# Third mixture of a four-layer gated decoder: gate weights by way of memory, and later and earlier places for the steps around it

## The reference, cut to what matters

```python
x = x + tanh(g_xattn[2]) * _L2_xattn_ref(_layernorm(x), ctx, ...)   # product in the frequency domain (rfft, irfft)
x = x + tanh(g_ffn[2])   * _L2_ffn_ref(_layernorm(x), ...)          # the third mixture
x = x + tanh(g_xattn[3]) * _L3_xattn_ref(ctx, ctx, _layernorm(x), ...)
x = x + tanh(g_ffn[3])   * _L3_ffn_ref(_layernorm(x), ...)          # the last mixture
```

```python
scores = sigmoid(X @ gate_w.T)
_, idx = top_k(scores + bias, 4)
w = take(scores, idx); w = w / sum(w)
pos = cumsum(onehot(idx)) - 1; valid = pos < C        # C = 128 places per expert
h = silu(xe @ W1) * (xe @ W3);  ye = h @ W2           # per expert
out = sum over the 4 of ye * (w where valid) + silu(X @ sw1.T) * (X @ sw3.T) @ sw2.T
```

## Time and profile before

| | |
|---|---|
| median of 3 runs | 866.2 us (862.1 to 868.02) |
| the profiled execution | 867.06 us, its span 865.3 us |
| mean granted clock of TensorE | 0.939 |
| PE, DVE, POOL, ACT busy | 88%, 64%, 45%, 43% of the span |
| third mixture, first gate product to `out_back` | 536.03 to 728.22 us |
| DMA, mean over the span | 92 GB/s |

### The profile page before, as it was taken

The page is one execution under the profiler, slowest core; times in us unless marked ns, Lnnn a source line. Parts: engine busy times, 40 slices in busy tenths (PEclk is TensorE's granted clock), DMA queues, the critical chain, the costliest instruction groups (busy, mean ns, idle before and its releaser), DMA issues.

```text
span 865.3 us, 13644 instructions
## 1 busy us (share of the span) xinstructions
PE 759.5 (88%) x3936; PEld 539.0 (62%) x3936; DVE 553.4 (64%) x1813; ACT 375.8 (43%) x834; POOL 390.4 (45%) x381
## 2 busy tenths in 40 slices
PE   6989889999999878976979787999989989798995
PEld 3467767676767546654969786565645544555663
DVE  3377877777788378862633575978776655344554
ACT  0234344444445435625545334547455565313441
POOL 2000024544546434363674343655445665253772
PEclk8799989999999969966999998999999999899999
DMA  5021899930000121014677651000330000013325
GB/s 146 1 62 50 267 333 332 333 88 0 1 1 1 53 57 30 21 47 146 172 208 211 195 167 50 10 1 1 83 101 14 13 10 17 10 41 78 101 70 146
DMA packets 74394, 79.34 MB, mean 92 GB/s; under 512 B 17769, under 2 KB 61424, under 8 KB 74194
## 3 DMA queue, kind: packets, MB, share of 16 engines
q1 hardware_dynamic: 68112, 69.49, 27.8%
q0 software_dynamic: 5024, 8.54, 2.9%
q10 hardware_dynamic: 1186, 0.43, 0.2%
HBM read 40.48 MB, written 39.85 MB: 93 GB/s over the span
## 4 chain that ended last, share of the span: by engine, by line
PE 60%; DVE 22%; issue 7%; POOL 4%; ACT 3%; DMA 3%; SPq 1%; ACTq 0%; DVEq 0%; POOLq 0%
PE psum L1186 54%; PE psum L1635 1%; POOL s L754 1%; DVE hb L2328 1%; DVE hb L2329 1%; DVE hb L2326 1%; DVE mr L1984 1%; DVE const L1940 1%; POOL s L732 1%; PE psum L1245 1%; DMA chosen<-in_mask_1x1xSxS_ik 1%; DVE wk L1941 1%; PE psum L1373 1%; DVE l_lo L1900 1%; DMA l_hi<-y 1%
## 5 line engine op out<-in xcount | busy, mean ns | idle before, releaser
L1186 PE MATMUL psum<-xt_hi,wa_hi 128*128 128x512 f32 x272 | 129.0, 474 | 9.7 <-DVE hb L2329 5.0
L691 POOL TENSOR_TENSOR h_lo<-hb,h_hi 128x512 fp32r<-128x512 f32 x68 | 87.7, 1293 | 83.1 <-ACT h_hi L920 82.8
L759 POOL DMA_INDIRECT y<-xn x93 | 92.2, 992 | 64.7 <-DVE xn L2076 33.6
L902 ACT ACTIVATE hb<-psum 128x512 f32<-128x512 f32 x136 | 81.0, 596 | 86.3 <-PE psum L1186 85.7
L1186 PE MATMUL psum<-xt_lo,wa_hi 128*128 128x512 f32 x272 | 108.4, 399 | 0.0
L686 POOL TENSOR_TENSOR hb<-hb,wsb 128x512 f32<-128x512 f32 x64 | 82.3, 1286 | 56.6 <-DVE hb L2326 51.5
L662 POOL TENSOR_TENSOR rstd<-veps,neghalf 128x4 f32<-128x4 f32 x20 | 20.3, 1017 | 130.0 <-DVE veps L1878 129.6
L1186 PEld LDWEIGHTS psum<-xt_hi,wa_hi 128*128 128x128 f32 x272 | 52.7, 194 | 31.6 <-DVE hb L2329 9.5
L2326 DVE TENSOR_TENSOR hb<-hb,psum 128x512 f32<-128x512 f32 x68 | 46.0, 684 | 40.0 <-ACT hb L902 29.5
L1186 PE MATMUL psum<-hb,wa_hi 128*128 128x512 f32 x136 | 70.9, 602 | 0.5 <-POOLq L688 0.5
L1186 PEld LDWEIGHTS psum<-xt_lo,wa_hi 128*128 128x128 f32 x272 | 52.5, 193 | 16.2 <-issue 7.5
(11 more groups left out here) (353 smaller groups left out, 1706.9 us busy)
## 6 DMA issues: line engine op xcount, KB each, us to landing
s<-l_lo SPq DMA_DIRECT2D x20, 1386.0 KB, 16.5
l_hi<-in_pack SPq DMA_DIRECT2D x24, 322.0 KB, 3.4
l_lo<-in_pack SPq DMA_DIRECT2D x22, 322.0 KB, 3.4
xn<-s SPq DMA_DIRECT2D x93, 66.0 KB, 2.0
stage<-in_pack SPq DMA_DIRECT2D x13, 256.0 KB, 2.7
y_in<-y SPq DMA_DIRECT2D x8, 256.0 KB, 3.8
l_hi<-y SPq DMA_DIRECT2D x8, 256.0 KB, 4.9
stage<-in_L_ffn_W SPq DMA_DIRECT2D x12, 128.0 KB, 2.4
```

The lines of the kernel that those rows point to most:

```text
L691: pool.tensor_tensor(h_lo[:, k % 3, :], hb[:, k % 4, :], h_hi[:, k % 3, :].bitcast(F32), ALU.subtract).then_inc(q["hlo_pool"], 1)
L759: pool.indirect_dma_start(y3, bass.IndirectOffsetOnAxis(xe3[:, j % XE, 128:129].bitcast(I32), 0), xe3[:, j % XE, 0:128], None, bounds_chec ...
L902: act.activation(hb[:, k % 4, :], G[k % 2][:, :], ACT.Silu).then_inc(q["sg_done"], 1)
L1186: return pe.matmul(o, l, r, start=start, stop=stop, skip_group_check=True)
```

## The change

- Gate weights: `route_end` writes the weights in f32 (`wfin`) in place of the three parts; `comb_in` transposes them in f32, 32 rows; `pre_comb` copies them to `wt2` and ACT writes them to memory (`wd`). For each unit with routed experts SP reads two rows back, each repeated over 64 partitions, into `wsb`. The pick on PE and the copy on ACT are gone; POOL waits for the transfer's semaphore.
- Order of units: the shared expert is unit 0 of a batch, the routed pairs are 1 to 16.
- The last mixture's weights are issued by ACT at unit 40 (`L3_AT`).
- Table `CH`: from `pt` on each step is one index later (`norm` stays at 7); `COUNT_PE` and `CH_LATER` follow.
- Tables of stage 5: routing of the next batch closer together and ended sooner, `fft_steps` later.
- Table `FFT1`: the first batch's routing closer together, `comb5` inside the loop.

```diff
+L3_AT = 40
-            back1=42, rows5=42, upd1=43, xt5=44, low5=45, logits5=46, score5=47, choose5=48, cum5=49, end5=50)
+            back1=42, rows5=42, upd1=43, xt5=44, low5=44, logits5=45, score5=46, choose5=47, cum5=48, end5=48, comb5=49)
-CH = dict(mom6=0, scl6=3, xt6=4, scores=5, exp=6, norm=7, pt=7, ptc=8, val=8, up=9, scl7=12, xt7=13, logits=14, top=15,
-          choose=16, cum=17, slots=18, scatter=19)
+CH = dict(mom6=0, scl6=3, xt6=4, scores=5, exp=6, norm=7, pt=8, ptc=9, val=9, up=10, scl7=13, xt7=14, logits=15, top=16,
+          choose=17, cum=18, slots=19, scatter=20)
-CH_LATER = {(2, "cum"): 78, (2, "slots"): 78, (2, "scatter"): 79}
+CH_LATER = {(2, "cum"): 79, (2, "slots"): 79, (2, "scatter"): 80}
-COUNT_PE = [SH_AT + t for t in (17, 18, 19)]
+COUNT_PE = [SH_AT + t for t in (18, 19, 20)]
...
+        wt2 = nc.alloc_sbuf_tensor_at("wt2", [32, 512], F32, offset=at["comb_t"])
+        wfin = nc.alloc_sbuf_tensor_at("wfin", [128, TB, 32], F32, offset=at["chl"])
...
-            return c, 20 + c, 40 + c
+            return (c - 1, 15 + c, 31 + c) if c else (48, 49, 50)
...
-        ROUTE_AT = {0: (5, 6, 7, 9, 10, 11, 11, 12, 12), 2: (8, 8, 8, 8, 8, 9, 10, 11, 12)}
-        WEIGH_AT = {0: 13, 2: 14}
-        COMBT_AT = {0: 15, 2: 16}
-        PE_XN, PE_LOGITS, PE_RUN, PE_COMB = {0: 0, 2: 2}, {0: 1, 2: 5}, 11, {0: 12, 2: 13}
+        ROUTE_AT = {0: (5, 6, 7, 9, 10, 11, 11, 12, 12), 2: (8, 8, 8, 8, 8, 9, 9, 9, 10)}
+        WEIGH_AT = {0: 13, 2: 11}
+        COMBT_AT = {0: 15, 2: 13}
+        PE_XN, PE_LOGITS, PE_RUN, PE_COMB = {0: 0, 2: 2}, {0: 1, 2: 5}, 8, {0: 12, 2: 10}
...
-                return 2 + b, (4, 7, 8, 11, 10, 13)
+                return 2 + b, (6, 9, 12, 14, 14, 16)
...
-            sp.wait_ge(q["x_done"], x_num(4, 3))
-            for i, w in enumerate(("routed_w1", "routed_w2", "routed_w3")):
-                sp.dma_start(pk3[:, :, F3 * i:F3 * i + F3], a["L3_ffn_" + w].rearrange("e d h -> d e h")).then_inc(d_wl, 16)
-            sp.dma_start(hi_flat[:, 0:512], a["L3_ffn_shared_w1"][0]).then_inc(d_wl, 16)
...
+            for b in range(B):
+                sp.wait_ge(d_wt2, WT2 + 16 * (b + 1))
+                for c in range(ROUTED[2]):
+                    w = b * ROUTED[2] + c
+                    if w >= 3:
+                        sp.wait_ge(q["w_used"], w - 2)
+                    for e in range(2):
+                        sp.dma_start(wsb[64 * e:64 * e + 64, w % 3, :],
+                                     wd[b, 2 * c + e:2 * c + e + 1, :].broadcast_to([64, S])).then_inc(d_w1[w % 3], 16)
...
-                    w = b * ROUTED[2] + c
-                    pool.wait_ge(q["wcopy_done"], w + 1)
+                    w = b * ROUTED[2] + c - 1
+                    pool.wait_ge(d_w1[w % 3], WB2[w % 3] + 32 * (w // 3 + 1))
...
+                if l == 2:
+                    if b:
+                        act.wait_ge(d_wt2, WT2 + 16 * b)
+                    act.activation(wt2[:, :], T[0:32, :], ACT.Copy).then_inc(q["combt_done"], 1)
+                    act.wait_ge(q["combt_done"], fnum(l, b))
+                    act.dma_start(wd[b], wt2[:, :]).then_inc(d_wt2, 16)
+                    return
...
-                    act.activation(wsb[:, w % 3, :], W[0][:, :], ACT.Copy).then_inc(q["wcopy_done"], 1)
...
+            def load_layer3():
+                act.wait_ge(q["x_done"], x_num(4, 3))
+                for i, w in enumerate(("routed_w1", "routed_w2", "routed_w3")):
+                    act.dma_start(pk3[:, :, F3 * i:F3 * i + F3], a["L3_ffn_" + w].rearrange("e d h -> d e h")).then_inc(d_wl, 16)
+                act.dma_start(hi_flat[:, 0:512], a["L3_ffn_shared_w1"][0]).then_inc(d_wl, 16)
+                act.dma_start(hi_flat[:, 512:1024], a["L3_ffn_shared_w2"][0]).then_inc(d_wl, 16)
+                act.dma_start(sw3, a["L3_ffn_shared_w3"][0].rearrange("(c h) d -> h c d", c=4)).then_inc(d_wl, 16)
...
-                    pre_comb(2, 0)
+                        if at1(g, "comb5"):
+                            pre_comb(2, 0)
...
-                            if l == 2:
-                                high(l, b, c)
-                            elif k >= 1:
+                            if l == 2 and k == L3_AT:
+                                load_layer3()
+                            if l != 2 and k >= 1:
...
+                for k in range(TB if l == 2 else 0):
+                    last = pe.transpose(T[0:32, 128 * k:128 * k + 128], wfin[:, k, :], ident)
...
-                if l == 2 and k - CB[2] >= 1:
-                    pe.wait_ge(q["wcopy_done"], sum(1 for i in range(k - CB[2]) if i % NC[2] < ROUTED[2]))
-                if c == 0:
+                if l == 0 and c == 0:
...
-                    last = mm(W[0 if l == 2 else k % 2][:, :], pick, comb_t[0:3 * N_EXP[l], b % 2, :], True, True)
+                    last = mm(W[k % 2][:, :], pick, comb_t[0:3 * N_EXP[l], b % 2, :], True, True)
...
-                    comb_in(2, 0)
+                        if at1(g, "comb5"):
+                            comb_in(2, 0)
...
-                    link(dve.tensor_tensor(w_, w_, m_, ALU.mult))
+                    dve.tensor_tensor(wfin[:, :, :], w_, m_, ALU.mult).then_inc(q["comb_done"], 1)
+                    return
...
+    wd = nc.dram_tensor("wd", (B, 32, S), F32, kind="Internal").ap()
```

More of the change, by code:

```diff
@@ L210, in link, with build @@
         self.eng.wait_ge(self.sem, self.n)
-def build(nc, a, out, s1, s3, y3, stages=8):
+def build(nc, a, out, s1, s3, y3, wd, stages=8):
     with ExitStack() as ctx:
@@ L308, in build @@
         d_x = [sem(f"d_x{b}") for b in range(B)]
+        d_wt2, WT2 = d_wnat, 16 * 4
+        WB2 = [16 * len(range(i, NB1, WS)) for i in range(3)]
         d_stage = [sem(f"d_stage{i}") for i in range(2)]
@@ L1421, in comb_in @@
                 use_t()
-                for k in range(TB):
+                for k in range(TB if l == 2 else 0):
+                    last = pe.transpose(T[0:32, 128 * k:128 * k + 128], wfin[:, k, :], ident)
+                for k in range(0 if l == 2 else TB):
                     last = pe.transpose(T[:, :].bitcast(BF16)[0:rows, 128 * k:128 * k + 128], chl[:, k, 0:rows], ident_bf[:, :])
@@ L1449, in gu @@
                 last = product(U[k % 2][:, :], us)
[L1450 to L1452 removed]
+                if l == 0 and c == 0:
                     pe.wait_ge(q["combt_done"], fnum(l, b))
[L1454 to L1459 removed]
+                if l == 0 and c < ROUTED[l]:
+                    pick = pair_sel[:, 2 * c:2 * c + 2, :].rearrange("p e i -> p (e i)")
+                    last = mm(W[k % 2][:, :], pick, comb_t[0:3 * N_EXP[l], b % 2, :], True, True)
                 last.then_inc(q["u_done"], 1)
```

25 lines of the change are left out of this document (3 added, 22 removed).

## The result

The changed kernel takes 877.63 us (median of 4 runs, 874.33 to 879.0), the kernel before 864.15 us beside it (861.82 to 868.02): a ratio of 1.0135, 95% interval 1.0099 to 1.0170. It is slower; the forecast was 857, with a range of 845 to 868. The profiled execution of the changed kernel takes 877.17 us, its span 875.4.

What follows compares the result with a forecast made beforehand. It took TensorE and VectorE to be near a bound in the first batch and later batches to wait. Terms -21.7 + 3 - 1 - 2.3 - 1.5 + 3 + 6 + 5.3 = -9.2 took 867.06 to 857.9, less 0.9: 857 us, range 845 to 868.

Steps and rivals of the forecast that it cites:

- The picks and the wait for them: Third mixture, TensorE: 64 picks (14.7 us) and the waits for ACT's copy (7) go, -21.7 us.
- +3, -1, -1.5 and +3 around it: Third mixture: VectorE nearly full +3; ACT's copies gone -1; shorter wait for probabilities -1.5; packed routing on VectorE +3.
- the +3 for the packed units: Batches' packed routing: some 6 us of VectorE between two products stall TensorE, +3 us (0 to +6).
- the gain is swallowed: Rival, chance 0.22: packed unit stalls at +6, ACT's issue shows in full at +11; 865 us.
- ACT's issue: Unit 40: six weight issues hold ACT 10.8 us, delaying scaled rows; +6 us (0 if VectorE's backlog hides it, +11 if all shows).
- Gate weights at nothing: Each unit's gate weights read from memory: round of 4.7 us, three buffers cover it, cost 0; upper bound 58 us.
- the slower rival: Rival, chance 0.10: gate weights' round sets the third mixture's pace, POOL waits for a buffer; some 886 us.
- The first weights arrive near 541.4: Start of third mixture: first gate weights land near 541.4 with a 2.4 us landing; unit 1 loses 0.5 us.
- First batch packed: First batch's routing: first gate product 2.8 us earlier (1.1 hi/lo operations, 1.7 loop order); -2.3 after unit 1's loss.
- The chain one unit on: Attention chain one unit later: the 3.7 us wait before the probabilities shrinks, -1.5 us (0 to -3.7).
- After the mixture: Behind the third mixture: copy and logits ahead of out_back +1.5, last cumulation behind a shared down product +3.8; +5.3 us.
- The signs that it named: Pitch 1.78, no copy wait; POOL's transfer wait only at unit 1; TensorE idle near 42; late cumulation; first gate product near 533.

Runs made afterwards that it cites:

- e16_picks: Kernel before without picks and copies, gate weights via memory, last mixture's weights spread, first gate weights early, row additions later, shared expert first, Fourier steps moved; ratio 1.0015.
- e8_best: Changed kernel with weight issues spread, first gate weights ahead and additions later, last two chains' old steps, second chain's scatters from unit 64; 854.69 us against 867.16, ratio 0.9879.
- e10_route: e8_best with the routing of batches 1 to 3 at its old places, chains unchanged; ratio 0.9860 to the kernel before.
- e14_all: e8_best plus a third up buffer, the first chain's scatters from unit 62, and old routing places for batches 1 to 3; ratio 0.9863 to the kernel before.
- e1_spread: Changed kernel, but ACT issues the last mixture's six weight transfers one at a time, at units 40 to 55; ratio 1.0034 to the kernel before.
- e5_rows: Changed kernel with the first three units' gate weights ahead of the result rows, and VectorE adding those rows at units 5 and 7; ratio 1.0105 to kernel before.
- e2_first: Changed kernel, but SP issues the first three routed units' gate weights before the second mixture's result rows of batches 2 and 3; ratio 1.0159 to kernel before.
- e12_first_batch: Kernel before with only the first batch's routing packed, its transposition and copy inside the loop, three-part weights kept; ratio 0.9978.
- e3_chain: Changed kernel with the attention chain's table (CH, CH_LATER, COUNT_PE) at its old numbers; ratio 1.0132 to the kernel before.
- e6_tail: Changed kernel, but the chains of batches 2 and 3 (counted from 0) take their old steps; ratio 1.0041 to the kernel before.
- e15_issue: Kernel before with one edit: ACT, not SP, issues the last mixture's six weight transfers in a row at unit 40; ratio 1.0105.

## Why the prediction was wrong

**The picks and the wait for them (-21.7, with +3, -1, -1.5 and +3 around it: -18.2).** What leaves TensorE was right: 64 picks, no wait for a copy, a quiet unit of 1.78. The step that failed is "I give back half of the first batch's 3.7 us and a quarter of the second's, 3 us rounded up", with the +3 for the packed units. It took VectorE's share of a whole batch for the measure of how near a bound it is. Where every other loss is repaired the stage of the profile gains 6.0 us, alone 5.6 (which the timed runs of e16_picks don't show), so some 12 of the 18 went back. They did not go back by VectorE's share: against the kernel before, e8_best is 1.6 us longer in b1 and only 0.7 shorter in b4, where VectorE is half busy, and 3.5 and 3.4 shorter in b2 and b3. The +3 for the packed units was no large part of it: with the old places the stage is 0.8 shorter (e10_route).

What the runs show is that the waits trade places: TensorE, VectorE and POOL wait for each other in one chain of buffers (gate product, silu, VectorE's product, POOL's product, down product). Putting the picks back cost 4.5 us, and a third up buffer turned 12 us of waits for VectorE into waits for POOL and the probabilities, for 1.1 us. That bursts of other work on VectorE set when the chain moves on is argued, not shown. This is the rival "the gain is swallowed", which had 0.22 and was priced by two other terms. By the prediction's own terms e8_best, which mends the issue, the start and the end, should gain 21 us (9.2 + 6 + 0.5 + 5.3); it gains 10.5 in the timed runs and 6.7 behind the first return. What holds the chain in e14_all, where 9.3 us of waits for POOL stay in ten places, is open.

**ACT's issue (+6).** The mechanism and its place were right: ACT held, its scaled rows late, a clock that falls. The size was not. The step took SP's 10.8 us for the issue and 1 us for the clock. With the gate weights beside them it was 14.0 us, the wait 8.1 in place of 5, and the lower clock 5.8 us, 4.1 more than before, in place of 1 more. Against e1_spread units 38 to 44 take 30.2 us in place of 16.8, 13.4 more, and the whole kernel 8.8 by the ratios, since e1_spread loses 4.4 at its end; on the kernel before, with no gate weights, the same issue costs 7.0 on the stage. The clock's part was a matter of luck, as the last section shows. The bound of +11 ("if all shows") left the clock out.

The Trainium skill, "DMA: Bandwidth & Descriptors", section "Issuing engines are not separate DMA queues", calls the sequencer's time for a DMA usually small beside the transfer. The trace agrees for one transfer at a time (0.70 to 0.85 us for 1 MB that lands after 8.0 us) and differs for six in a row (14.0 us, of which a large one lands after 11.7). So the prediction was right to set the rows above the rule here, and missed what the two together say: spread the issues.

**Gate weights at nothing (0, and 0.5 at the start).** Right but for the start. The transfers land in 2.9 us (2.4 assumed), and in the changed kernel the three-unit cover holds everywhere else but for 0.8 us; the slower rival that had the weights' round set the pace is refuted. The cover gets thin once the rest is mended: POOL waits 8.1 us for these transfers in e8_best and 12.4 in e14_all, at unit 4 and beside the last mixture's weights. In e8_best 2.7 us of it reach TensorE (units 4 and 44), in e14_all 1.8 (unit 4). "The first weights arrive near 541.4" failed: the 2.4 us is the median of twelve loads, ten of them with nothing close ahead, and here four result loads were landing in the same queue. The other two of the twelve, behind large loads, had landed after 12.6 and 9.0 us in the trace that the prediction read. It cost 3.4 us (b1 of the changed kernel against e5_rows), and e2_first shows why the order alone could not mend it.

**First batch packed (-2.8 ahead of unit 1).** Right in size: from 2.0 us behind the last return to 0.5 ahead of it, 2.5. Its split wasn't: e12_first_batch keeps the hi and lo operations, to which 1.1 of it were put, and has all of the 2.5.

**The chain one unit on (-1.5).** The wait for the probabilities fell by 2.5. Without the shift it is 8.8 us beside the packed routing (e3_chain), which the prediction had half said, and 5.6 beside the old one (e16_picks); with it 1.5 beside the old one (e10_route). So the shift pays for more than the packed routing's damage, though e16_picks and e10_route differ in POOL's scatters too.

**After the mixture (+5.3).** Right: 5.6 on the end stretch, 5.3 on the cumulation, and 5.4 back with the last two chains at their old places.

In sum, some 12 us of the picks' gain did not come, the issue cost 7 more than said and the start 3: 22 us, against 21.1 between the forecast -9.2 and the +11.9 behind the first return, or 18.9 counted from the last return. That the first two agree so closely is luck: each of them carries some us of clock. The signs that it named did come, so each loss was seen, and the sum was still wrong in sign, because the one large gain was priced as work removed and not as what the engines around it would let through.

## What to carry to other kernels

Work taken from the busiest engine is worth what its neighbours in the buffer chain let through: before counting it, ask for each wait of the others whether it would move along; a cheap test is to put the work back as a dummy and see whether the time notices. Don't issue a row of large transfers from an engine that others wait for: one at a time the six here cost 0.36 to 0.85 us each, in a row they held ACT for 11.1 to 14.0 us. When a new user joins a queue of transfers, list what stands ahead of it, and who else waits for what is now behind it.

## What was not expected of the hardware

After TensorE's stop of 8.10 us in the changed kernel the granted clock is at the lower level for 11.6 us. In e6_tail the same stop, ended by the same wait and followed by the same matmuls, has 5.4 us of it:

```profile
657.84:669.44 11.60, 11.60 (x35) 8.58 (x35) 5.32 (x21) 5.68 (x9) 4.63 (x4) 0.50 0.42 134
669.44:683.00 13.56, 13.56 (x68) 8.88 (x68) 10.66 (x30) 4.86 (x10) 8.62 (x10) 1.00 0.32 99
```

```profile
653.21:658.57 5.36, 5.36 (x18) 4.27 (x18) 2.98 (x4) 3.42 (x6) 2.76 (x3) 0.50 0.73 224
658.57:670.00 11.43, 10.58 (x56) 6.59 (x54) 8.59 (x32) 4.59 (x8) 5.64 (x5) 1.00 0.28 90
```

Nor does a longer stop mean a longer low clock: 5.7 us behind 9.23 in e2_first, 14.1 behind 8.71 in e5_rows, 3.4 behind 6.91 in e15_issue, where full-width products came first. So in these profiles neither the length of the stop nor the matmuls behind it tell how long the clock stays low, and the 5.8 us that it cost in the changed kernel could as well have been 2.7. That is some 3 us by which a single profile of the same code can differ at this one place.
